# Attention and SwiGLU on one core: the context moved by DMA, and a prologue with other fillers

## The reference

```python
x = L0_attn_hidden_states                     # (4, 1024, 128)
xn = _layernorm(x, axis=-1)
q = (xn @ Wq.T + bq).reshape(b, t, 16, 8)     # k, v: 4 heads of 8; q and k are rotated (rope)
scores = jnp.einsum('bthd,bshd->btsh', q, k) * scale
probs = jax.nn.softmax(scores, axis=2)
context = jnp.einsum('btsh,bshd->bthd', probs, v).reshape(b, t, DIM)
attn = context @ Wo.T + bo
h = jax.nn.silu(xn @ wg.T) * (xn @ wu.T)      # weights are int32 / 127
return x + attn + h @ wd.T
```

## Time and profile before

| | |
|---|---|
| runs | 753.49, 754.30 and 754.54 us, median 754.3 |
| the profiled execution | 752.47 us, of which the span (first to last instruction) is 750.3 |
| busy share | PE 96%, DVE 91%, ACT 83%, POOL 30% |
| granted TensorE clock | 0.998 of full speed on average |
| chain that ended last | PE 75%, DVE 16%, ACT 6% |
| context transposes (L1244) | 124 matmuls, 19.4 us busy |
| staging transposes (L1252) | 28 matmuls, 4.6 us busy |

### The profile page before, as it was taken

The page is one execution under the profiler, slowest core; times in us unless marked ns, Lnnn a source line. Parts: engine busy times, 40 slices in busy tenths (PEclk is TensorE's granted clock), DMA queues, the critical chain, the costliest instruction groups (busy, mean ns, idle before and its releaser), DMA issues.

```text
span 750.3 us, 13756 instructions
## 1 busy us (share of the span) xinstructions
PE 718.9 (96%) x4914; PEld 216.2 (29%) x4914; DVE 682.7 (91%) x1265; ACT 624.2 (83%) x1305; POOL 227.0 (30%) x372
## 2 busy tenths in 40 slices
PE   7899999999999999999999999999999999999987
PEld 6332222222322222222322222232322222232222
DVE  6899999999999999999999999999999999999931
ACT  5638989888888988888888888889788888989886
POOL 3776552256331662112111212211121211202100
PEclk9999999999999999999999999999999999999999
DMA  9524331110311131010111101011111101110030
GB/s 298 176 65 110 117 118 33 33 34 2 117 34 33 33 115 35 5 43 19 33 33 33 33 24 43 2 34 33 33 33 33 33 2 33 33 33 2 2 85 29
DMA packets 30723, 38.26 MB, mean 51 GB/s; under 512 B 5600, under 2 KB 20448, under 8 KB 30400
## 3 DMA queue, kind: packets, MB, share of 16 engines
q1 hardware_dynamic: 27680, 30.18, 14.1%
q0 software_dynamic: 1440, 4.72, 1.7%
q10 hardware_dynamic: 1536, 2.49, 1.0%
HBM read 23.28 MB, written 11.53 MB: 46 GB/s over the span
## 4 chain that ended last, share of the span: by engine, by line
PE 75%; DVE 16%; ACT 6%; issue 2%; DMA 1%; SPq 0%; ACTq 0%; DVEq 0%
PE acc_ps L1229 29%; PE banks L1123 20%; DVE mx L946 13%; PE banks L1143 10%; PE banks L1096 7%; ACT probs L719 5%; PE banks L1236 4%; PE banks L1244 3%; PE banks L1063 1%; PE banks L1069 1%; DMA y_all<-in_x 1%; PE banks L1279 1%; PE banks L1252 1%; DVE stats L853 1%; DVE row_max L952 0%
## 5 line engine op out<-in xcount | busy, mean ns | idle before, releaser
L946 DVE TENSOR_REDUCE mx<-banks 128x1 f32<-128x512 f32 x1024 | 637.6, 682 | 27.1 <-PE banks L1123 24.0
L719 ACT ACTIVATE probs<-banks 128x512 f32<-128x512 f32 x1024 | 549.1, 606 | 91.3 <-PE banks L1143 86.1
L1143 PE MATMUL banks<-qc,kc 51*128 51x512 bf16 x1024 | 304.8, 382 | 10.6 <-ACT probs L719 5.5
L1123 PE MATMUL banks<-ka,qa 48*128 48x512 bf16 x1024 | 302.0, 382 | 7.1 <-DVE mx L946 6.9
L1229 PE MATMUL acc_ps<-probs,v_grp 128*32 128x512 f32 x2048 | 272.7, 605 | 1.2 <-ACT probs L719 1.0
L1123 PEld LDWEIGHTS banks<-ka,qa 48*128 48x128 bf16 x1024 | 67.2, 94 | 292.0 <-DVE mx L946 247.6
L577 POOL TENSOR_TENSOR neg_max<-row_max,nought 128x16 bf16<-128x16 f32 x32 | 7.1, 222 | 315.5 <-DVE row_max L952 310.2
L1143 PEld LDWEIGHTS banks<-qc,kc 51*128 51x128 bf16 x1024 | 64.5, 94 | 44.2 <-ACT probs L719 40.9
L1096 PE MATMUL banks<-xn_T,w_ffn 128*128 128x256 f32 x188 | 65.8, 434 | 0.0
L1229 PEld LDWEIGHTS acc_ps<-probs,v_grp 128*32 128x32 f32 x2048 | 40.3, 108 | 85.5 <-ACT probs L719 59.1
L601 POOL TENSOR_TENSOR gated<-gu 128x256 f32<-128x256 f32 x48 | 35.2, 734 | 73.7 <-ACT gu L808 73.7
(11 more groups left out here) (110 smaller groups left out, 349.3 us busy)
## 6 DMA issues: line engine op xcount, KB each, us to landing
qa<-q_rows SPq DMA_DIRECT2D x28, 192.0 KB, 3.5
qc<-q_rows SPq DMA_DIRECT2D x56, 96.0 KB, 2.6
q_rows<-part POOLq DMA_DIRECT2D x18, 256.0 KB, 4.2
ka<-k_later SPq DMA_DIRECT2D x24, 96.0 KB, 2.2
kc<-k_later SPq DMA_DIRECT2D x24, 96.0 KB, 2.2
out<-y_all SPq DMA_DIRECT2D x16, 128.0 KB, 2.0
y_all<-in_x SPq DMA_DIRECT2D x3, 512.0 KB, 12.3
k_rows<-part SPq DMA_DIRECT2D x6, 256.0 KB, 3.0
```

Source lines behind the costliest of these rows:

```text
L719: nc.scalar.activation(probs[:, s % SLOTS, j, :], banks[:, score_bank(g, G * s + j), :], ACT.Exp, scale=SCALE).then_inc(exp_done, 1)
L946: nc.vector.tensor_reduce(out=mx[:, h, col, k:k + 1], in_=ps, op=ALU.max, axis=AX.X).then_inc(max_done, 1)
L1123: nc.tensor.matmul(ps, qa[par][rows, j // 2, t * P:(t + 1) * P], ka[par][rows, k * W:(k + 1) * W], start=True, stop=True).then_inc(a_ready, 1)
L1143: nc.tensor.matmul(banks[:, score_bank(g, u), :], kc[par][rows, kt * P:(kt + 1) * P], qc[par][rows, h, j // 2, :], start=True, stop=True). ...
```

## The change

Of the context: after each copy to `acc_sb` SyncE moves for each head the 8 rows of the context to their place in `ctx_T` (now two batches deep) and the row of sums to a DRAM tensor `sums_rows` (`move_context`, 8 DMAs). When a batch is whole, the sums are loaded as 128x128 (`load_sums`), inverted by VectorE (`invert`, in the slot of `GATE` 2, step 10 of groups 4, 8 and 12), stored, and loaded back spread over the 8 rows of each head (`load_inverse`); VectorE multiplies 128x512 once for each half (`divide`, in the slot of `GATE` 2 of groups 5, 6, 9, 10, 13 and 14). For the last batch the sums are moved straight to 8 rows each of `last_sums` (the columns of ones are now 8), and inverted there: `divide_rest` for 96 rows of half 1 and `divide(6)` for half 0, both in group 15. The jobs `CTX` and `STAGE`, their VectorE operations and ScalarE's copy are gone; the end of the last group still goes by transposes, for its own 32 rows alone. Twelve of the output stores are issued in group 15 ahead of its own moves.

Of the prologue: the first input tile comes in two halves, the second on ScalarE's queue ahead of the identity; the third gate/up pair of the first chunk stands behind maximum 1 and not 6; eight more products that nobody reads stand behind maximum 3; and the first query projections stand behind maxima 7 and 9 and not 8 and 10. `root` has four operations and not five ahead of `shift`.

```diff
-PE_XN, PE_FFN, PE_Q1, PE_V = (2, 4, 12, 14, 16, 18), 6, (8, 10), (20, 22)
+PE_XN, PE_FFN, PE_Q1, PE_V = (2, 4, 12, 14, 16, 18), 1, (7, 9), (20, 22)
-JOB_AT = {1: (DOWN, 0), 2: (DOWN, 1), 3: (GATE, 0), 4: (UP, 0), 5: (NEG_T, 1), 6: (GATE, 1), 7: (UP, 1), 8: (CTX, 0),
-          10: (GATE, 2), 11: (UP, 2), 13: (NEG_T, 0), 16: (CTX, 1)}
+JOB_AT = {1: (DOWN, 0), 2: (DOWN, 1), 3: (GATE, 0), 4: (UP, 0), 5: (NEG_T, 1), 6: (GATE, 1), 7: (UP, 1),
+          10: (GATE, 2), 11: (UP, 2), 13: (NEG_T, 0)}
-    return {9: (STAGE, u), 12: (PROJ, 2 * u), 14: (PROJ, 2 * u + 1)}
+    return {12: (PROJ, 2 * u), 14: (PROJ, 2 * u + 1)}
...
-            load_x(0, slice(0, NT))
+            load_x(0, slice(0, HT))
             load_x(1, slice(0, HT))
...
+            def move_context(g, h):
+                b = g // KV
+                sp.wait_ge(acc_copied, NH * g + h + 2)
+                if b > 1 and g % KV == 0:
+                    sp.wait_ge(o_ps, 2 * NH * (b - 1))
+                for j in range(G):
+                    head = g % KV * G + j
+                    rows, n = slice(head * HD, (head + 1) * HD), (h * H + head) * W
+                    sp.dma_start(ctx_T[rows, b % 2, h, :], acc_sb[VC * j:VC * j + HD, h, :]).then_inc(moved[h], 16)
+                    if b < B - 1:
+                        sp.dma_start(sums_rows[b:b + 1, n:n + W],
+                                     acc_sb[VC * j + HD:VC * j + HD + 1, h, :]).then_inc(moved[h], 16)
+                    else:
+                        sp.dma_start(last_sums[rows, h, :],
+                                     acc_sb[VC * j + HD:VC * j + 2 * HD, h, :]).then_inc(moved[h], 16)
...
             def group(g, par, left):
                 if left > 1:
                     sp.wait_ge(pv_done, STEPS * g + SLOTS)
                     load_parts(g + 1, qc[1 - par], kc[1 - par], qc_loaded[1 - par])
+                if g > 0:
+                    move_context(g - 1, 1)
                 load_neg(g, 1, par)
+                if g % KV == 0 and g > 0:
+                    load_sums(g // KV - 1)
+                if g % KV == 1 and g > KV:
+                    load_inverse(g // KV - 1)
+                if left == 1:
+                    store_out(0, 2 * OUTS - 4)
+                move_context(g, 0)
...
         def _(act):
+            act.dma_start(y_all[:, HT:NT, :],
+                          x[0].rearrange("(t p) d -> p t d", p=P)[:, HT:NT, :]).then_inc(x_in[0], 16)
             act.dma_start(ident[:, :], identity).then_inc(ident_in, 16)
...
-                nc.vector.tensor_tensor(nw[:, tiles], nw[:, tiles], rc[:, tiles], ALU.mult).then_inc(newton, 1)
+                nc.vector.scalar_tensor_tensor(nw[:, tiles], nw[:, tiles], -0.5, rc[:, tiles], ALU.mult,
+                                               ALU.mult).then_inc(newton, 1)
                 dve.wait_ge(newton, n + 3)
-                nc.vector.tensor_scalar(nw[:, tiles], nw[:, tiles], -0.5, 1.5, ALU.mult, ALU.add).then_inc(newton, 1)
+                nc.vector.scalar_tensor_tensor(rstd[:, tiles], nw[:, tiles], 1.5, rc[:, tiles], ALU.add,
+                                               ALU.mult).then_inc(newton, 1)
                 dve.wait_ge(newton, n + 4)
-                nc.vector.tensor_tensor(rstd[:, tiles], nw[:, tiles], rc[:, tiles], ALU.mult).then_inc(newton, 1)
-                dve.wait_ge(newton, n + 5)
...
+            def invert(b):
+                dve.wait_ge(sums_loaded, 16 * (b + 1))
+                nc.vector.reciprocal(row_sums[:, :], row_sums[:, :]).then_inc(inverted, 1)
+            def divide(u):
+                b, h = u // 2, u % 2
+                if b < B - 1:
+                    dve.wait_ge(spread_in[h], 16 * (b + 1))
+                    by = spread
+                else:
+                    dve.wait_ge(moved[h], MOVES * NG)
+                    nc.vector.reciprocal(last_sums[:, h, :], last_sums[:, h, :]).then_inc(last_inverted, 1)
+                    dve.wait_ge(last_inverted, 2)
+                    by = last_sums
+                nc.vector.tensor_tensor(ctx_T[:, b % 2, h, :], ctx_T[:, b % 2, h, :], by[:, h, :],
+                                        ALU.mult).then_inc(divided, 1)
...
                 if a == PE_FFN:
+                    pe.wait_ge(select_done, 4)
                     first_ffn(FC - 1)
+                if a == 3:
+                    keep_busy(IDLE_RING, banks[:, 3, :])
...
             def project_out(u, ps):
                 if u < 2 * OUTS - 2:
-                    pe.wait_ge(ctx_T_done, u // 2 + 1)
+                    pe.wait_ge(divided, u // 2 + 1)
                 else:
+                    pe.wait_ge(rest_divided, 1)
                     pe.wait_ge(end_T_done, u % 2 + 1)
```

More of the change, by code:

```diff
@@ L340, in attention_swiglu @@
         y_done = sem("y_done")
[L341 to L345, removed]
+        moved = sems("moved", NH)
+        sums_loaded = sem("sums_loaded")
+        inverted = sem("inverted")
+        inverse_stored = sem("inverse_stored")
+        spread_in = sems("spread_in", NH)
+        last_inverted = sem("last_inverted")
+        divided = sem("divided")
+        rest_divided = sem("rest_divided")
         o_ps = sem("o_ps")
@@ L385, in attention_swiglu @@
         END_T = HT // 2
+        MOVES = 16 * 2 * G
+        END_ROWS = slice(P - G * HD, P)
         @block.sync
@@ L478, in _, with store_out, load_sums, store_inverse @@
                 load_twins(b)
+            def store_out(first, last):
+                for u in range(first, last):
+                    sp.wait_ge(o_done, u + 1)
+                    sp.dma_start(out[u // 4, (u % 4) * HW:(u % 4 + 1) * HW, :].rearrange("(t p) d -> p t d", p=P),
+                                 y_all[:, u * HT // 2:(u + 1) * HT // 2, :]).then_inc(out_stored, 16)
+            def move_context(g, h):
[13 more added lines that the diff above has]
+                                     acc_sb[VC * j + HD:VC * j + 2 * HD, h, :]).then_inc(moved[h], 16)
+            def load_sums(b):
+                for h in range(NH):
+                    sp.wait_ge(moved[h], MOVES * KV * (b + 1))
+                sp.dma_start(row_sums[:, :], sums_rows[b].rearrange("(p c) -> p c", c=P)).then_inc(sums_loaded, 16)
+            def store_inverse(b):
+                sp.wait_ge(inverted, b + 1)
+                sp.dma_start(inverse_rows[b].rearrange("(p c) -> p c", c=P), row_sums[:, :]).then_inc(inverse_stored, 16)
+            def load_inverse(b):
+                sp.wait_ge(inverse_stored, 16 * (b + 1))
+                if b > 0:
+                    sp.wait_ge(divided, NH * b)
+                rows = inverse_rows[b].rearrange("(h e w) -> h e w", h=NH, e=H)
+                for h in range(NH):
+                    sp.dma_start(spread[:, h, :], rows[h].unsqueeze(1).to_broadcast([H, HD, W]))                        .then_inc(spread_in[h], 16)
             def group(g, par, left):
@@ L502, in _ @@
                 group(g, g % 2, min(3, NG - g))
[L504 to L507 removed]
+            store_out(2 * OUTS - 4, 2 * OUTS)
             sp.wait_ge(out_stored, 16 * 2 * OUTS)
@@ L1010, in job @@
                     add_attention(n, ps)
+                elif kind == GATE and n == FC - 1:
+                    if g % KV == 0 and g > 0:
+                        invert(g // KV - 1)
+                    if g in OUT_AT:
+                        divide(OUT_AT[g][12][1] // 2)
+                elif kind == NEG_T and g == NG - 1:
+                    divide_rest()
+                    divide(OUTS - 2)
             def group(g, order):
```

104 lines of the change are left out of this document (37 added, 67 removed).

## The result

| | before | changed |
|---|---|---|
| median of 5 runs | 753.98 us (753.39 to 754.54) | 759.05 us (757.27 to 759.55) |
| ratio of the runs | 1 | 1.0065, 95% interval 1.0053 to 1.0078 |
| profiled execution | 752.47 us, span 750.3 | 759.05 us, span 756.9 |

A forecast was written before the change was run, and what follows sets the result against it. Bound: a 2.48 us TensorE-ScalarE loop in steps without a job, TensorE's work in steps with one. Terms -4.5 -1.1 +1.9 +1.2 +0.7 +1.3 -0.4 -1.4 +4.5 = +2.2, giving 756.5 us; likeliest 755.8 to 758.5, 8 in 10 within 750.2 to 760.

The forecast's parts named there:

- Transposes taken out: Groups 0 to 14: 30 steps without context transposes give 0.15 each, -4.5 us; six steps 9 without staging, -1.1.
- the loop of 2.48: Steps without a job: the wait loop between TensorE and ScalarE lets none fall under 2.48 us.
- rival B: Whole kernel: TensorE is the bound, so context passes (19.4 us) and some 4 for staging fall out; 731 us, chance 0.03.
- VectorE: Output and inversion groups: six new multiplications cost +1.9 us, three 128x128 reciprocals +1.2; bounds 0 and +4.5 together.
- my walk through the ring: Steps 10 to 13 through four banks: 0.32 us late per multiplication, 0.26 and 0.14 per reciprocal.
- SyncE's queue in group 0: Group 0: moves make the load of the negated maxima 1.2 us late against 0.5 slack; +0.7 (0 to +1.5), once.
- Start: Prologue: later identity +1.3 us, shorter Newton step -0.4, filled waits -1.4; together -0.5.
- +1.3 - 0.4: Prologue: the identity's later landing costs 1.3 us, the shorter Newton step gives back 0.4.
- The filled waits: Prologue, about 30 to 32 us: moved up/gate products and eight idle products fill TensorE's wait, -1.4 us (0 to -2).
- Tail: Last group: output product 12 waits for moves, reciprocal and multiplication; +4.5 us, bounds +0.6 and +6.5, the largest term.
- rival C: Last group: the tail's wait also lowers TensorE's clock, about 3 us more; 759.5 us, chance 0.15.
- its own row on the start of the program: Prologue of the old kernel: granted clock 0.53 between 30 and 32 us after a thin stretch, cited for rival C.

The follow-up runs named there:

- e1_group0: Changed kernel with group 0's eight moves of half 0 issued behind the load of the negated maxima for group 1: 755.93 us, ratio 1.0031.
- e6_no_fill: Changed kernel without the eight unread products behind maximum 3: 760.83 us, ratio 1.0104.
- e4_tail_busy: Changed kernel with twenty unread identity products in front of output product 12's wait in the last group: 758.24 us, ratio 1.0059.
- e3_product_late: Changed kernel with the last group's output products 12 and 13 in steps 14 and 15, not 12 and 14: 755.37 us, ratio 1.0024.
- e12_group0_busy: Changed kernel with eight unread identity products before group 1's first scores, ahead of their wait for the negated maxima: 757.91 us, ratio 1.0069.
- e7: Changed kernel with the edits of e1_group0, e2_stores_behind, e3_product_late and e5_ident_first together: 749.07 us, ratio 0.9941.
- e9: The kernel of e7 with the six 128x512 multiplications moved from VectorE to GpSimd as well: 747.50 us, ratio 0.9923.
- e10: The kernel before with the change's prologue edits alone: 752.50 us, ratio 0.9991.
- e11: The kernel of e9 with ScalarE copying the transposed first tile between its sums and squares of tile 1: 746.47 us, ratio 0.9908.
- e2_stores_behind: Changed kernel with all 16 output stores at the end of SyncE's list, behind the last group's moves: 756.54 us, ratio 1.0043.
- e8: Changed kernel with the six 128x512 multiplications of batches 0 to 2 moved from VectorE to GpSimd: 756.76 us, ratio 1.0045.
- e5_ident_first: Changed kernel with the identity issued ahead of the first input tile's second half on ScalarE's queue: 758.95 us, ratio 1.0075.

## Why the prediction came out as it did

The sign was right and its main reason too: the wait of the tail is the largest term. The size was short: +5.1 on the medians of five runs and +6.6 on the profiled executions, against +2.2. The profiled execution of before was 1.5 under its median, that of the changed kernel on it. By its own steps:

- **Transposes taken out**: right. Steps 8 and 16 went from 2.75 to 2.59 (forecast 2.60), step 9 of the output groups from 2.66 to 2.48. The argument that ScalarE's copy of the accumulator, and not the loop of 2.48, holds these steps was the one that mattered: a bound of TensorE's work alone (rival B, 731) was 28 us off.
- **VectorE**: right in sum, by errors that cancel. The multiplication costs 0.25 a group (0.08 in step 11, 0.18 in step 13) and not 0.32, 1.5 and not 1.9. The reciprocal of 128x128 takes 0.94 and not 0.85. It costs 0.36 in steps 11 and 13 of groups 4 and 8, another 0.27 in step 15 of group 4, behind the end of my walk through the ring, and 0.54 in steps 11 and 12 of group 12: 1.5 and not 1.2.
- **SyncE's queue in group 0**: the step that failed. I had +0.7 for a load that is 1.2 late with 0.5 of slack. The landings in the traces date the pieces; each is counted from its kernel's first product with the values, changed kernel against e1_group0. The second load is issued 1.4 late (38.00 against 36.59), as worked out. What I left out is that the traffic pushed back with it is still under way: it took 2.78 to land and not 1.95, 0.8 more. The slack was 0.4 and not 0.5. 1.4 + 0.8 - 0.4 = 1.8 is the 1.88 by which the scores started late. The second thing left out is the clock: the wait brought TensorE to the 1.2 GHz level for 6.8 us, some 1.6 more. The measured term is +3.45, where I had bounded it at 1.5.
- **Start**: the sum is nearly right (-0.75 against -0.5), in part by luck. The identity came 1.9 later and not 1.3, and the transposes started after 12.5 as forecast. The first maxima are 0.97 late where +1.3 - 0.4 says 0.9, but by another path: the identity holds the start only by the 0.30 us that ScalarE's copy waited for the transposes. Right behind it stands ScalarE's work on input tile 1, which the split also delays, and which was not in the prediction; so with the identity in at 3.3 to 3.5 little or nothing was won (first values product at 60.65, 59.40 and 58.96, against 59.48). The filled waits gave 1.7 and not 1.4, of which the eight products 1.3 (e6_no_fill).
- **Tail**: the chain was right to 0.3 us: moves from 729.97 (forecast 729.8), divided at 740.82 (740.6), though the reciprocal took 3.35 and not 2.9. ScalarE ran dry at 736.7 (736.5). It had work again at 742.74 and not 741.8, and then stood another 1.20, both because TensorE was at the low level. That is rival C, and e4_tail_busy shows 1.40 of it. So the term of +4.5 measured +6.51. I had put it beside the forecast as another case with 0.15; by its own row on the start of the program it belonged in the sum.

Measured, 759.05 lies just over the likeliest case's own range (755.8 to 758.5), inside the wide one (750.2 to 760), and nearest rival C's 759.5. C is right in what it says of the tail, and only half of its 3 us: the rest of the way is group 0. That its number comes so near is luck.

## What to carry to other kernels

Put new transfers into a queue behind those that someone waits for, and ahead of those that nobody does: two moves in SyncE's list are worth 3.45 and 2.4 us here. Neither alone makes the change win (755.93 and 756.54); with output products 12 and 13 later as well it does (749.07). When a sum has a new wait of TensorE in it (here 1.49 and 5.79 us), price what comes behind it at the low clock as well, and remember that shortening such a wait without closing it may leave a part of that price in place (e3_product_late). When a filled wait is used to measure the clock, look whether the fillers overran it (e12_group0_busy). An engine that lists its work in order can hide which input is late: before a transfer is brought forward, follow every engine between it and its use.

## What the runs showed of the hardware

- VectorE's reciprocal takes 200 ns for 8 columns, 941 for 128 and 3353 for 512, and 3343 for 96 rows of 512: 6.2 to 6.3 ns a column, and 96 rows take as long as 128. The slope of 5.4 from two tiny sizes was too low.
- GpSimd multiplies 128x512 in 1.28 us where VectorE takes 0.69, and VectorE's maxima beside it were not slowed (steps 9 and 10 kept their 2.48 and 2.70).
- Moves of 8 rows take SyncE 0.63 us each to issue, moves of one row 0.42, and output stores 0.50 (0.53 with the gap).
- The load of the negated maxima (two DMAs of 6 KB) landed 1.95 to 2.02 us after its second issue where little traffic stood ahead of it (the kernel before, e1, e7, e9, e10 and e11), and 2.26 to 2.80 where the pushed-back stores and loads did (the changed kernel, e2 to e6, e8 and e12).
- The same list of instructions gave group 0 lengths from 44.35 to 46.54 us in seven profiles. Which wait brings the clock down is not a matter of its length alone: it fell with waits of 1.18 us (e6_no_fill) and of 1.45 to 1.53 (e8, the changed kernel, e4, e3), and stayed at 1.00 with waits of 0.95 (e2_stores_behind) and 1.34 (e5_ident_first).
